# Factorisation-machine layers in one kernel: the spread input is laid out with one HBM row per partition, and its second chunk no longer waits for the weights as a whole

## What is computed

```python
x0 = xk = inputs                                  # (512, 39, 16)
for idx, (W, b) in enumerate([(w0, b0), (w1, b1), (w2, b2)]):
    z = relu(einsum('bhd,bkd,hks->bsd', x0, xk, W) + b[None, :, None])   # s = 128
    if idx != 2:
        xk = z[:, :64, :]
        direct.append(z[:, 64:, :])
    else:
        direct.append(z)
logit = sum(concatenate(direct, axis=1), axis=-1)
```

## Time and profile before

| | |
|---|---|
| median of 3 executions | 617.9 us (617.33 to 618.14) |
| profiled execution, its own time | 616.5 us |
| its span, first to last instruction | 614.7 us |
| mean granted TensorE clock | 0.983 |
| PE busy | 572.0 us (93% of the span) |
| DVE, POOL, ACT busy | 510.2, 453.3, 339.8 us |
| loaded and stored by DMA | 121.55 MB, 198 GB/s over the span |

### The profile page before, as it was taken

The page is one execution under the profiler, slowest core; times in us unless marked ns, Lnnn a source line. Parts: engine busy times, 40 slices in busy tenths (PEclk is TensorE's granted clock), DMA queues, the critical chain, the costliest instruction groups (busy, mean ns, idle before and its releaser), DMA issues.

```text
span 614.7 us, 7442 instructions
## 1 busy us (share of the span) xinstructions
PE 572.0 (93%) x1952; PEld 370.9 (60%) x1952; DVE 510.2 (83%) x471; ACT 339.8 (55%) x372; POOL 453.3 (74%) x196
## 2 busy tenths in 40 slices
PE   2677849999999999999999999999999999999977
PEld 0354536666666666666666666666666666666644
DVE  2659838989888998989898898988899898989854
ACT  1435444746475574746566474647557474656632
POOL 0263745969879696978969696987969697896965
PEclk9799969999999999999999999999999999999989
DMA  8994999999699695959789595959869595970000
GB/s 275 232 290 126 230 286 228 286 245 267 152 275 203 209 230 182 229 134 278 171 244 229 184 227 162 255 132 277 200 213 224 188 227 138 277 167 0 1 2 34
DMA packets 17406, 121.55 MB, mean 198 GB/s; under 512 B 2058, under 2 KB 2058, under 8 KB 5108
## 3 DMA queue, kind: packets, MB, share of 16 engines
q1 hardware_dynamic: 16992, 120.59, 76.8%
q10 hardware_dynamic: 404, 0.84, 0.5%
HBM read 120.90 MB, written 0.52 MB: 198 GB/s over the span
## 4 chain that ended last, share of the span: by engine, by line
PE 85%; DMA 11%; DVE 1%; issue 1%; ACT 1%; SPq 1%; ACTq 0%
PE z L438 85%; DMA field_spread<-w2s 5%; DMA fields<-x_fields 4%; DMA field_spread<-w0s 2%; SPq L197 1%; ACT hi L481 1%; DVE w_lo L317 0%; DVE exact L262 0%; DVE raw L262 0%; DVE d_raw L262 0%; DVE sums L308 0%; ACT maps L496 0%; ACT z L504 0%; ACTq L529 0%; SPq L191 0%
## 5 line engine op out<-in xcount | busy, mean ns | idle before, releaser
L373 POOL TENSOR_TENSOR lo<-raw,hi 128x1024 fp32r<-128x1024 f32 x192 | 453.1, 2395 | 155.9 <-ACT hi L481 141.7
L481 ACT ACTIVATE hi<-raw 128x1024 fp32r<-128x1024 f32 x192 | 203.2, 1059 | 135.1 <-DVE raw L262 130.4
L438 PE MATMUL z<-exact,w_exact 128*128 128x512 f32 (+2 forms) x544 | 258.4, 600 | 11.8 <-DVE exact L262 11.8
L262 DVE TENSOR_TENSOR raw<-field_spread,maps 128x1024 f32<-128x1024 f32 x192 | 228.2, 1215 | 35.8 <-ACT maps L496 23.8
L438 PE MATMUL z<-hi,w_hi 128*128 128x512 f32 (+1 forms) x480 | 211.0, 440 | 26.0 <-ACT hi L481 26.0
L438 PE MATMUL z<-lo,w_hi 128*128 128x512 f32 (+1 forms) x480 | 178.4, 463 | 1.0 <-POOL lo L373 1.0
L438 PE MATMUL z<-hi,w_lo 128*128 128x512 f32 (+1 forms) x448 | 178.8, 399 | 0.0
L438 PEld LDWEIGHTS z<-exact,w_exact 128*128 128x128 f32 (+2 forms) x544 | 104.2, 192 | 94.5 <-issue 70.5
L438 PEld LDWEIGHTS z<-hi,w_hi 128*128 128x128 f32 (+1 forms) x480 | 91.4, 190 | 61.8 <-issue 22.4
L438 PEld LDWEIGHTS z<-lo,w_hi 128*128 128x128 f32 (+1 forms) x480 | 90.6, 189 | 54.4 <-issue 38.3
L262 DVE TENSOR_TENSOR exact<-field_spread,maps 128x1024 f32<-128x1024 f32 x96 | 116.6, 1214 | 2.4 <-DMA field_spread<-x_spread 2.4
(11 more groups left out here) (11 smaller groups left out, 22.4 us busy)
## 6 DMA issues: line engine op xcount, KB each, us to landing
field_spread<-x_spread SPq DMA_DIRECT2D x80, 1024.0 KB, 16.0
fields<-x_fields SPq DMA_DIRECT2D x16, 1280.0 KB, 7.8
fields<-x_fields SPq DMA_DIRECT2D x16, 768.0 KB, 4.6
field_spread<-w1s SPq DMA_DIRECT2D x1, 896.0 KB, 14.7
field_spread<-w2s SPq DMA_DIRECT2D x1, 896.0 KB, 30.9
field_spread<-w0e ACTq DMA_DIRECT2D x1, 585.0 KB
out<-sums SPq DMA_DIRECT2D x2, 256.0 KB, 2.1
w_exact<-w1e SPq DMA_DIRECT2D x1, 384.0 KB, 16.6
```

The lines of the kernel that those rows point to most:

```text
L262: nc.vector.tensor_tensor(ring, spread[0:rows, 2 * k:2 * k + tiles, :], by[0:rows, :].unsqueeze(1).to_broadcast([rows, tiles, COLS]), ALU. ...
L373: nc.gpsimd.tensor_tensor(lo[0:rows, slot % LO_RING, :, :], raw[0:rows, raw_slot % RAW_RING, :, :], hi[0:rows, slot % HI_RING, :, :].bitca ...
L438: mm = nc.tensor.matmul(z[layer][:, :], w[0:rows, :], part[0:rows, :], start=(step == 0 and p == 0), stop=(step == len(order) - 1 and p == ...
L481: nc.scalar.activation(hi[0:rows, slot % HI_RING, :, :], products, ACT.Copy).then_inc(hi_ready, 1)
```

## The change

Three things change. `x_spread` in HBM has one row per partition (128 per chunk in place of 16), and a load of a fifth is a plain copy of 128 rows of 8 KB. The raw weights are staged so that those of layer 0 lie in the first fifth of the half of chunk 1, those of layer 1 in the second, and those of layer 2 in the last; each load of chunk 1 waits for the splits of what lies under it. And ACT splits the weights of layer 2 behind the maps of layer 1 in place of ahead of layer 0's split.

```diff
-        w_staged = [stage(SPLIT_TILES[n]) for n in range(3)]
-
+        w0e_parts = stage(2 * EXACT_TILES[0])
         w0s_parts = stage(2 * SPLIT_TILES[0])
-        w0e_parts = stage(2 * EXACT_TILES[0])
+        w_staged = [stage(SPLIT_TILES[0])]
+        assert staged_tiles * OUT <= 4 * COLS
+        staged_tiles = 4 * COLS // OUT
+        w_staged.append(stage(SPLIT_TILES[1]))
+        assert staged_tiles * OUT <= 8 * COLS
+        staged_tiles = 16 * COLS // OUT
+        w_staged.append(stage(SPLIT_TILES[2]))
...
             def load_spread(c, par, q):
-                base = x_spread[c, 0:1, 4 * q:4 * q + 4, :]
-                src = bass.AP(tensor=base.tensor, offset=base.offset,
-                              ap=[[TILES * COLS, 2 * COPIES], [0, HALF // COPIES], [1, 4 * COLS]])
-                sp.dma_start(field_spread[:, par, 4 * q:4 * q + 4, :], src).then_inc(spread_loaded[par][q], 16)
+                sp.dma_start(field_spread[:, par, 4 * q:4 * q + 4, :],
+                             x_spread[c, :, 4 * q:4 * q + 4, :]).then_inc(spread_loaded[par][q], 16)
...
             load_weights(2, w2e, w2s)
+            sp.wait_ge(w0e_summed, 1)
+            sp.wait_ge(weights_lo, WEIGHTS_LO[0])
+            load_spread(1, 1, 0)
+            sp.wait_ge(weights_lo, WEIGHTS_LO[1])
+            for q in range(1, PARTS - 1):
+                load_spread(1, 1, q)
             sp.wait_ge(weights_lo, WEIGHTS_LO[2])
-            for q in range(PARTS):
-                load_spread(1, 1, q)
+            load_spread(1, 1, PARTS - 1)
...
                 if first:
                     copy_fields(1)
-                    act.wait_ge(w_staged_loaded[2], 16)
-                    weights_split_hi(2)
                 if more:
                     split_hi(0, i, d, split_of(0))
                 act.wait_ge(lo_used, place("SD", i, d, 0)[0])
                 spread_maps(1, maps2, direct[HALF:OUT, :], z1_evacuated)
+                if first:
+                    act.wait_ge(w_staged_loaded[2], 16)
+                    weights_split_hi(2)
...
-    x_spread = np.repeat(pair.transpose(0, 2, 1, 3), COPIES, axis=1)
+    x_spread = np.repeat(pair.transpose(0, 2, 1, 3), HALF, axis=1)
```

More of the change, by code:

```diff
@@ L18 @@
 TILES = (FIELDS + 1) // 2
-COPIES = 16 // 2
 FIRST_SHIFTS = 2
```

## The result

The changed kernel takes 601.06 us (600.73 to 601.46, 4 runs) against 617.92 before: the ratio is 0.9729, with a 95% interval of 0.9712 to 0.9746. That is 16.9 us faster, inside the stated range; the forecast was 20.3 us faster, at 597.6.

The account below looks back on a forecast made before the run. PE bounds the kernel (93% busy, alone from 85.02 us); only loads ahead can be won. 23.9 + 14.7 + 2.0 + 8.7 + 14.7 + 35.1 = 99.1 against 119.36 saves 20.3: 617.9 to 597.6 us, range 594 to 604.

Parts of the forecast that it names:

- The rate: Spread loads in the new layout: 425 GB/s in place of 228, so 2.5 us per fifth in place of 4.65.
- The stall of chunk 1: In chunk 1, ACT's 13.47 us wait for chunk 2's fields and PE's 10.50 us standing were to go.
- the early issue: Chunk 1's spread fifths go out as split waits allow; chunk 2's fields land by 55, before ACT asks at 62.
- The moved split: Chunk 0, layer 1's end to layer 2: 8.67 us against 8.84, with 3.0 us idle PE; the move wins nothing itself.
- The clock behind it: The idle PE ahead of chunk 0's layer 2 could halve the clock again: up to 1.7 us more.
- The start: Chunk 0's layer 1 starts on PE at 23.9, costs 14.7 plus 2.0 us for the clock, and ends at 40.6.
- DVE starts at 21.45: Chunk 0, layer 1: the first fifth lands by 20.9, so DVE starts when layer 0's maps are ready, before at 22.98.
- PE starts at 23.9: Chunk 0, layer 1: PE starts 2.45 us behind DVE, against 25.43 before.
- the half clock: Chunk 0, layer 1: after 3.9 us idle PE, 1.65 or 3.35 us lost; 2.0 taken, ends 0 and 3.35.
- The rate that stays: Rival: spread loads stay at 228 GB/s and only the earlier issue helps, 9.5 us, 608.4 us; chance 10%.
- that price: For the unchanged rate: 8.1 us idle DMA filled, chunk 2's fields at 75.3, PE stands 2.4 us: 608.4 us.
- The slower rival: Rival: 8 times as many different HBM bytes slow the spread loads; under 174 GB/s each chunk pays; chance 3%.

Follow-up runs that it names:

- layout_only: The kernel before with the layout alone (128 rows in HBM, plain copy): 595.1 us, ratio 0.9616.
- w2_split_early: The changed kernel with ACT's split of layer 2's weights put back ahead of layer 0's split: 595.22 us, ratio 0.9635 to the kernel before.
- layout_and_move: The kernel before with the new layout and ACT's split of layer 2's weights moved behind the maps, still one wait for chunk 1's five loads: 600.33 us, ratio 0.9698.
- rows_16x8: The changed kernel, its 128 different HBM rows read as 16 groups of 8, as the old load was: 609.79 us, ratio 0.9869 to the kernel before.
- halves: The changed kernel with each spread load as two plain copies of 64 partitions: 611.34 us, ratio 0.9909 to the kernel before.
- waits_only: The changed kernel with the old layout (16 rows, each read 8 times): 611.44 us, ratio 0.9908 to the kernel before.
- waits_no_move: Staging and split waits alone, old layout, ACT's split of layer 2's weights where it was: 609.76 us, ratio 0.9869 to the kernel before.
- one_row_128: The changed kernel with all 128 partitions filled from one HBM row, output not the reference's: 598.42 us, ratio 0.9690 to the kernel before.

## Why the prediction was right, and what it missed

**The rate: right.** 419 and 424 GB/s against 425 assumed. DVE has no wait for the spread left.

**The stall of chunk 1: right, and for one reason more than given.** It is gone. The prediction let the early issue take the credit; `layout_only` shows that the faster loads remove it alone, as chunk 1's loads then go out at 45.22 and land in time.

**The moved split: mechanism right, size nearly.** The way from layer 1's end to layer 2 was put at 8.67 us and is 8.69 (51.03 - 42.34); the idle PE was put at 3.0 and is 2.85. That it would hide without the move was said, and `w2_split_early` shows it. The clock behind it was left out of the sum, as "up to 1.7 us more": it did fall. Layer 2 of chunk 0 took 67.24 - 51.03 = 16.21 us against 14.69, 1.52 more. That is one mis-sized term.

**The start: the term that was mis-sized most.** "DVE starts at 21.45" and "PE starts at 23.9" took the end of the first layer 0 from one execution. There it ended at 20.0 and hid behind a wait for a load that lasted until 22.98. Once that wait was gone the end itself counted, and it scatters: PE began layer 1 at 23.43 to 27.07 over the six profiles with fast loads that start alike, at 25.87 in this one. That is 1.97 us more. The first layer 1 then took 16.47 us against 16.7 forecast: the half clock cost 1.76 us, where 2.0 had been picked between ends of 0 and 3.35. That this term fits is in part luck.

**The end: not foreseen.** Ahead of the last layer 2 PE idles 3.85 us in both kernels, and the half clock behind it lasted about 3.3 us before, when that layer took 16.51 us, and until about 583 us, some 5.8 us, after: 17.77 us, 1.26 more. Stretch 577 to 584, after:

```profile
577.00:584.00 7.00, 6.73 (x14) 4.04 (x15) 7.00 (x8) 4.36 (x5) 6.80 (x3) 0.56 0.00 1
```

`layout_only` (16.58) and `w2_split_early` (16.53) have the short form. `layout_and_move` has the short form there too (16.62), and the long one behind its gap in chunk 0 (68.17 - 50.44 = 17.73). What decides between the two stays open; the two layers together take about as long in both kernels, 33.98 and 34.35 us.

The sum over the profiles: 1.97 - 0.2 + 1.52 + 1.26 = 4.5 us, which is 20.3 less 15.8, the difference of the spans. Between the medians it is 3.4. Chunk 1 took the 35.09 us that were forecast.

**The rivals.** The rate that stays is what `rows_16x8`, `halves` and `waits_only` make of the kernel: 609.8, 611.3 and 611.4 us, where 608.4 was worked out. What failed in that price is the landing of chunk 2's fields: 75.3 us was worked out by filling 8.1 us of idle DMA time, and ACT got them at 77.20, 79.45 and 80.92 in the profiles of `waits_only`, `rows_16x8` and `waits_no_move`, with PE starting again 1.62 to 1.63 us behind. The gap ahead of layer 2, which the price also left out, lies ahead of that wait and is hidden by it. The slower rival had no part: 128 different rows read about as fast as one.

**The better version.** `layout_only` and `w2_split_early`, at 595.1 and 595.2 us, beat both kernels: 22.4 to 22.5 us off where the whole change takes 16.9.

## What to carry to other kernels

When a stretch shows all DMA engines busy but at half the rate of other loads, look at the form of the load, how many partitions one copy fills and in what groups, before looking at the bytes: a plain 128-partition copy here cost 2.5 us for 1 MB where the same bytes in 16 groups, or in two 64-partition copies, cost about 4.7. An order that was neutral while loads were late (1.0015) can cost 5 us once they are early; after a change that speeds up loads, ask of each wait and each one-off piece of work where it would now hide. And a landmark that lies hidden behind a wait is not a number to build a sum on: once the wait goes, its own scatter shows.

## What the runs showed of the hardware

- 128 partitions filled from one HBM row ran at 424 GB/s, from 128 rows 40 KB apart at 419 and 424. 16 groups of 8 partitions ran at 226, two copies of 64 partitions at 223.
- Early matmuls of the program ran at half pace (those of `hi` 0.43 us apart in place of 0.23) in a stretch whose granted clock is shown as 1.00. They did so until between 19.3 and 20.0 us in the changed kernel and until about 22 us in its second profile. In `w2_split_early`, with the same instructions up to there, they ran at full pace from 15.27 us.
- Behind 2.82 to 2.85 us of idle PE (chunk 0, layer 2) the granted clock was at half in the changed kernel, both times that it was profiled, and in `layout_and_move` and `one_row_128`; behind 1.55 us, in the kernel before, it did not.
